# A Mamba block with a routed expert layer on one core: residual through TensorE, second layer norm on ScalarE

## The chip, the cores and the metric

The kernel runs on one core of one Trainium2 chip, as a single launch. Its metric is the device time in microseconds. Before the change it is 2424.81 us, the median of 3 runs (2423.86 to 2426.68).

## The reference, cut to what matters

The input is 4 sequences of 2048 tokens with 256 channels, all in float32. A selective scan with a residual is followed by a mixture of experts with a residual. In short:

```
h = layernorm(x) * (1 + ca) + sa
xs, res = split(h @ in_proj.T)                  # 512 + 512 channels
xs = silu(causal_conv4(xs) + conv_b)
dt, B, C = split(xs @ x_proj.T)                 # 64, 16, 16
delta = softplus(dt @ dt_proj.T + dt_b)
state = exp(delta * A) * state + delta * xs * B # 512 channels x 16 states, along the tokens
y = sum_n(state * C) * silu(res)
x = x + ga * (y @ out_proj.T)                   # the residual of this case
h = layernorm(x) * (1 + cb) + sb                # the second layer norm of this case
x = x + gb * moe(h)                             # 7 routed experts (top 1) and 1 shared
```

`layernorm(v)` is `(v - mean) / sqrt(var + 1e-5)` over the 256 channels.

## The kernel before, in words

There are two stages. The first, `fused_program`, walks the 8192 tokens in 16 chunks of 512; four chunks make one sequence. It does everything but the routed experts. The second, `experts_program`, handles 70 tiles of routed tokens and is not touched.

Within a chunk the 512 x 16 states are laid out as 16 sets of 4 groups, each group 128 partitions by 512 tokens, so a chunk has 64 scans of 128x512. For every group ScalarE makes `exp(delta * A)` into one of three PSUM banks `dA` (L850), VectorE scans it (L973), and after the four groups of a set ScalarE saves the last state (L865) and GpSimd multiplies the set by C (L1279). The input `delta * xs * B` of ten sets is multiplied by VectorE (L960), of the six others by GpSimd (L1272). TensorE sums over the states with a 0/1 matrix (L590). The states live in a ring of 8 sets.

All other work is put into this frame as items. Each item has a kind, an index and a chunk offset: offset 1 is work ahead for the next chunk, offset -1 is work for the chunk before. The kinds are: T and XS, RS, CV, XP, DT, DB (turn, input projection in two halves, convolution, x projection, delta), SUM (sum over states of 128 channels, and its gate by silu(res)), OP (output projection, two halves of 256 tokens), T2, RB, GL, GT (turn of the second norm, its copy back, logits), A and B and Y (shared expert), SU (Silu of the convolution), SRS (Silu of `res` and of the shared expert's gate), L0 and L1 (logarithms for softplus), N and N2 (normalize), LN and LN2 (layer norm sums), R and R2 (rsqrt), DU (delta times u), IN (input of a shared set), RC, G, G0, GM0, GM1 (the small gate arithmetic).

The order on each engine is written out by hand in five lists: `plan` for TensorE (one list of items per set), `evict` for ScalarE and `vector` for VectorE (one per group in a set), `gps` for GpSimd (one per set) and `transfers` for the DMA queue of SyncE. Each engine walks its list in order and waits on semaphores. TensorE's results go to three banks: kinds in `VECTOR` ("SUM", "OP", "DB", "A", "Y") use bank 2, the others alternate between banks 0 and 1; a bank is taken again when its last holder has been read.

What the change touches: the output projection puts 2 x 4 matmuls of 128x256 into bank 2 (L535). VectorE adds the residual `xres` to it, 128x512 at a time (`residual`, L989). When both halves are there, VectorE makes the statistics (`layernorm2`, bn_stats L928 and bn_aggr L934), GpSimd turns them into `rstd2` and `shift2` with a power of -0.5 (`rsqrt2`, L1250 to L1255), and ScalarE normalizes (`normalize2`, L780).

Since `dA` has three banks, exponential u waits for scan u - 3:

```
if u >= ABANK:
    act.wait_ge(scan_done, NG * NSET * c + u - ABANK + 1)
```

## Time and profile before

| | |
|---|---|
| median of 3 runs | 2424.81 us |
| the profiled execution's own time | 2425.52 us |
| its span, first to last instruction | 2423.7 us |
| mean granted TensorE clock | 0.917 |
| TensorE busy | 2129.3 us, 88% |
| GpSimd busy | 1979.4 us, 82% |
| VectorE busy | 1948.4 us, 80% |
| ScalarE busy | 1346.9 us, 56% |

PE is TensorE's matmuls, DVE is VectorE, ACT is ScalarE, POOL is GpSimd, SP is SyncE. A busy time is a sum over stages: the scan stage lies between about 60 and 1888 us, a short stage that settles the routing follows, and from about 1974 us the routed experts run, where TensorE is the one that works most. "L12" is line 12 of the kernel's file. A row of the timeline gives start, duration, engine, line and operation, how many of it follow each other, and in brackets how long the engine sat idle before it and who ended that.

### The profile page before, as it was taken

How to read it: one execution, taken by the hardware profiler on the slowest of the kernel's cores; microseconds unless marked ns; L12 is line 12 of the kernel's file. 1: busy time of each engine (PE TensorE's matmuls, PEld its weight loads, DVE VectorE, ACT ScalarE, POOL GpSimd, SP SyncE). 2: the span in 40 equal slices, each digit the busy share in tenths (PEclk: the TensorE clock that was granted, in tenths of full speed). 3: DMA queues.
4: the chain of work that ended last, by engine and by line, in shares of the span. 5: the costliest groups of instructions: out<-in, count | busy, mean ns of one | idle time of the engine just before them, and what ended most of it. 6: DMA issues, size and time to landing. Idle time of an engine off the chain costs nothing. (4 is left out here: it accounts for less than half of the span.)

```text
span 2423.7 us, 31216 instructions
## 1 busy us (share of the span) xinstructions
PE 2129.3 (88%) x7668; PEld 1007.6 (42%) x7669; DVE 1948.4 (80%) x2114; ACT 1346.9 (56%) x2391; POOL 1979.4 (82%) x858
## 2 busy tenths in 40 slices
PE   8859898988989898989898989889875779999998
PEld 3214343443434343434343334434332456666565
DVE  4889999999999999999999999999999832222222
ACT  4657666667585767666666667675745212222221
POOL 1999999999989999999998999999899445555553
PEclk9868999899989898989899899999887889999999
DMA  6433242424242324343242424242422512222221
GB/s 175 137 101 98 78 106 65 104 74 117 77 102 72 98 74 103 83 101 103 75 111 74 108 68 117 80 103 69 98 69 53 208 42 87 86 87 85 84 85 47
DMA packets 148360, 224.35 MB, mean 93 GB/s; under 512 B 47187, under 2 KB 84577, under 8 KB 144098
## 3 DMA queue, kind: packets, MB, share of 16 engines
q1 hardware_dynamic: 134818, 182.40, 28.8%
q0 software_dynamic: 13376, 40.12, 5.5%
q8 instruction: 57, 0.93, 0.2%
q14 instruction: 109, 0.89, 0.1%
HBM read 99.46 MB, written 31.45 MB: 54 GB/s over the span
## 5 line engine op out<-in xcount | busy, mean ns | idle before, releaser
L1279 POOL TENSOR_TENSOR ring<-ring,reps 128x2048 f32<-128x2048 f32 x256 | 1154.7, 4530 | 42.6 <-ACT state L865 42.6
L973 DVE TENSOR_TENSOR_SCAN ring<-dA,state,ring 128x512 f32<-128x512 f32 x768 | 929.7, 1262 | 13.5 <-ACT dA L850 9.2
L850 ACT ACTIVATE dA<-d_rep,a 128x512 f32<-128x512 f32 x1024 | 690.1, 686 | 433.1 <-DVE ring L973 426.4
L1272 POOL TENSOR_TENSOR ring<-u_rep,reps 128x2048 f32<-128x2048 f32 x96 | 436.2, 4544 | 44.6 <-PE bank L590 44.5
L960 DVE TENSOR_TENSOR ring<-u_ps,reps 128x2048 f32<-128x2048 f32 x160 | 360.5, 2269 | 8.8 <-issue 4.9
L590 PE MATMUL bank<-ring,spread 128*32 128x512 f32 x2048 | 283.2, 703 | 42.4 <-POOL ring L1279 37.8
L561 PE MATMUL bank<-n,w1s 128*128 128x512 f32 x512 | 266.1, 657 | 61.1 <-DVE delta L941 38.5
L973 DVE TENSOR_TENSOR_SCAN ring<-dA,ring 128x512 f32<-128x512 f32 x256 | 293.7, 1201 | 11.5 <-ACT dA L850 10.4
L1553 DVE TENSOR_TENSOR hid<-z,sg 128x512 f32<-128x512 f32 x70 | 48.4, 692 | 295.6 <-ACT sg L1530 295.6
L1468 PE MATMUL z<-ring,hT 128*128 x560 | 262.2, 612 | 3.6 <-issue 2.1
L516 PE MATMUL bank<-xin,w_in 128*128 128x512 f32 x512 | 244.9, 619 | 8.3 <-ACT xin L701 8.3
L520 PE MATMUL bank<-xpad,w_conv 128*128 128x512 f32 x496 | 224.0, 601 | 8.9 <-ACT us L716 8.8
L527 PE MATMUL bank<-xdbl,w_dt 65*128 65x512 f32 x256 | 149.0, 680 | 68.9 <-ACT n L732 52.1
L1435 POOL DMA_INDIRECT out<-outr,cur x70 | 70.9, 1013 | 145.2 <-DVE outr L1546 138.2
L561 PEld LDWEIGHTS bank<-n,w1s 128*128 128x128 f32 x512 | 98.2, 205 | 195.6 <-issue 93.2
L590 PEld LDWEIGHTS bank<-ring,spread 128*32 128x32 f32 x2048 | 69.9, 127 | 233.4 <-issue 213.2
L580 PE MATMUL u_ps<-us,spread 32*128 32x512 f32 x320 | 161.6, 705 | 0.0
L516 PEld LDWEIGHTS bank<-xin,w_in 128*128 128x128 f32 x512 | 99.6, 198 | 131.9 <-issue 119.2
L1468 PEld LDWEIGHTS z<-ring,hT 128*128 128x128 f32 x560 | 101.9, 192 | 122.4 <-issue 122.3
L1530 ACT ACTIVATE sg<-z 128x512 f32<-128x512 f32 x70 | 41.8, 597 | 199.5 <-PE z L1468 199.5
L520 PEld LDWEIGHTS bank<-xpad,w_conv 128*128 128x128 f32 x496 | 92.1, 190 | 132.5 <-issue 110.8
L1486 PE MATMUL y_ps<-reps,hidT 128*128 x560 | 132.4, 379 | 0.8 <-ACT hidT L1519 0.8
(237 smaller groups left out, 2456.7 us busy)
## 6 DMA issues: line engine op xcount, KB each, us to landing
d_rep<-delta SPq DMA_DIRECT2D x1024, 64.0 KB, 2.0
reps<-bc_rows SPq DMA_DIRECT2D x128, 256.0 KB, 6.3
u_rep<-us SPq DMA_DIRECT2D x384, 64.0 KB, 2.0
xres<-in_x SPq DMA_DIRECT2D x16, 512.0 KB, 3.6
token_rows<-xpad SPq DMA_DIRECT2D x32, 256.0 KB, 2.4
token_rows<-xres SPq DMA_DIRECT2D x16, 512.0 KB, 2.9
xin<-in_x SPq DMA_DIRECT2D x15, 512.0 KB, 9.4
ring<-in_w SPq DMA_DIRECT2D x7, 1024.0 KB, 14.5
```

What stands on the lines that cost most here:

```text
L516: last = nc.tensor.matmul(ps_[:, :], t["w_in"][:, k, col:col + P], hT[:, k, :], start=(k == 0), stop=(k == KD - 1))
L520: last = nc.tensor.matmul(ps_[:, :], t["w_conv"][:, j, k, :], xpad[:, j, k:k + T], start=(k == 0), stop=(k == KCONV - 1))
L527: last = nc.tensor.matmul(ps_[:, :], t["w_dt"][:, j * P:(j + 1) * P], xdbl[0:DT_ROWS, :], start=True, stop=True)
L561: last = nc.tensor.matmul(ps_[:, :], t["w1s"][:, k, col:col + P], h2T[:, k, :], start=(k == 0), stop=(k == KD - 1))
L580: nc.tensor.matmul(u_ps[:, i % 2, :], t["spread"][DS * q:DS * q + DS].rearrange("p f d -> p (f d)"), us[DS * q:DS * q + DS, par, j, :], st ...
L590: last = nc.tensor.matmul(ps_[DS * q:DS * q + DS, :], t["gather"], hs[:, (SPC * j + q) % RING, n, :], start=(n == 0), stop=(n == NG - 1), ...
L850: nc.scalar.activation(dA[:, u % ABANK, :], d_rep[:, q, :], ACT.Exp, scale=t["a"][:, u:u + 1]).then_inc(da_ready, 1)
L960: nc.vector.tensor_tensor(hs[:, s % RING], u_ps[:, i % 2, :].unsqueeze(1).to_broadcast([P, NG, T]), b_rep[:, par, :].rearrange("p (g t) -> ...
L973: nc.vector.tensor_tensor_scan(hs[:, s % RING, g, :], dA[:, u % ABANK, :], hs[:, s % RING, g, :], state[:, u:u + 1] if m else 0.0, ALU.mul ...
L1272: nc.gpsimd.tensor_tensor(hs[:, s % RING], u_rep[:, i % UBUF, :].unsqueeze(1).to_broadcast([P, NG, T]), b_rep[:, par, :].rearrange("p (g t ...
L1279: nc.gpsimd.tensor_tensor(hs[:, s % RING, :, :], hs[:, s % RING, :, :], c_rep[:, par, :].rearrange("p (g t) -> p g t", g=NG), ALU.mult).th ...
L1468: last = nc.tensor.matmul(z[:, q % 2, half, :], hT[:, q % 2, i, :], t["w1r"][:, e, i, half * H:(half + 1) * H], start=(i == 0), stop=(i == ...
```

## The change

The residual is added by TensorE: each half of a projection begins with a matmul of the identity by `xres`, and the 4 matmuls of the projection accumulate onto it. Its bank is read by ScalarE, which writes the new `xres` and, as a second output, the sum of each row. ScalarE then does the rest of the second layer norm as well: `squares2` (VS0, VS1) makes the negative mean and the sum of squared deviations, `deviation2` (V2) makes rstd by Ln and Exp and the shift. VectorE's `residual` and `layernorm2` and GpSimd's `rsqrt2` go. All five lists get a new order, the six shared sets stay the same. In the part behind the last chunk, VectorE's first routing steps stand together behind SUM 3.

```diff
+                        pe.wait_ge(xres_loaded, 16 * f + 16)
                     for h in range(2):
+                        tt = 2 * j + h
+                        nc.tensor.matmul(ps_[:, h * D:(h + 1) * D], t["ident"][:], xres[:, tt, :], start=True, stop=False)
                         for k in range(KI):
-                            tt = 2 * j + h
                             last = nc.tensor.matmul(ps_[:, h * D:(h + 1) * D], res[:, (par + off) % 2, k, tt * P:(tt + 1) * P], t["w_out"][:, k, :],
-                                                    start=(k == 0), stop=(k == KI - 1))
+                                                    start=False, stop=(k == KI - 1))
...
+                elif kind == "OP":
+                    for h in range(2):
+                        tt = 2 * j + h
+                        last = nc.scalar.activation(xres[:, tt, :], ps_[:, h * D:(h + 1) * D], ACT.Copy, accum_out=sum2[:, tt:tt + 1])
+                    last.then_inc(x1_ready, 1)
...
+            def squares2(f, j):
+                part = slice(2 * j, 2 * j + 2)
+                act.wait_ge(x1_ready, 2 * f + j + 1)
+                nc.scalar.activation(nmean2[:, part], sum2[:, part], ACT.Copy, scale=-1.0 / D).then_inc(ln2_step, 1)
+                act.wait_ge(ln2_step, 2 * f + j + 1)
+                if not (known(f) and f == 0):
+                    act.wait_ge(a_made, KI * f)
+                for tt in range(2 * j, 2 * j + 2):
+                    last = nc.scalar.activation(n2[:, tt, :], xres[:, tt, :], ACT.Square, bias=nmean2[:, tt:tt + 1], accum_out=var2[:, tt:tt + 1])
+                last.then_inc(stats2_ready, 1)
+            def deviation2(f):
+                act.wait_ge(stats2_ready, 2 * f + 2)
+                nc.scalar.activation(rstd2, var2, ACT.Ln, bias=eps2[:, 0:1], scale=1.0 / D).then_inc(rstd2_step, 1)
+                act.wait_ge(rstd2_step, 2 * f + 1)
+                nc.scalar.activation(rstd2, rstd2, ACT.Exp, scale=-0.5).then_inc(rstd2_step, 1)
+                act.wait_ge(rstd2_step, 2 * f + 2)
+                for tt in range(TT):
+                    last = nc.scalar.activation(shift2[:, tt:tt + 1], nmean2[:, tt:tt + 1], ACT.Copy, scale=rstd2[:, tt:tt + 1])
+                last.then_inc(shift2_ready, 1)
...
-            5: [[], [], [(('CV', 3), 1)], []],
-            6: [[(('SU', 0), 1)], [], [(('HALO', 0), 2), (('RS', 0), 1)], []],
+            5: [[(('VS0', 0), -1)], [], [(('CV', 3), 1), (('SU', 0), 1)], []],
+            6: [[(('OP', 1), -1)], [], [], []],
...
-            def layernorm2(f):
...
-            def residual(f, j):
...
-            def rsqrt2(f):
```

What stands on ScalarE in chunk 1, around the Silu of the convolution (`us<-us 128x2048`). The rows `dA<-d_rep,a` are exponentials, `state<-ring` is the save behind the third of a set, `us<-bank1,cb` the eviction of a convolution, `xpad<-xpad` the halo. Before:

```order
L850 ACTIVATE dA<-d_rep,a 128x512 x3
L716 ACTIVATE us<-bank1,cb 128x512
L865 ACTIVATE state<-ring 128x4
L850 ACTIVATE dA<-d_rep,a 128x512 x2
L753 ACT_TABLE_LOAD
L753 ACTIVATE us<-us 128x2048
L764 ACT_TABLE_LOAD
L850 ACTIVATE dA<-d_rep,a 128x512 x2
```

And now:

```order
L734 ACTIVATE xres,ln2<-bank2 128x256 x2
L881 ACTIVATE dA<-d_rep,a 128x512
L786 ACTIVATE ln2<-ln2 128x2
L791 ACTIVATE n2,ln2<-xres,ln2 128x256 x2
L881 ACTIVATE dA<-d_rep,a 128x512 x2
L718 ACTIVATE us<-bank1,cb 128x512
L760 ACT_TABLE_LOAD
L760 ACTIVATE us<-us 128x2048
L771 ACT_TABLE_LOAD
L896 ACTIVATE state<-ring 128x4
```

The Silu with its two table loads moved from behind exponential 24 (the first of set 6) to behind exponential 22 (the third of set 5), into one gap with the eviction of the last convolution; the eviction of projection 0 and the first two Squares stand before it.

What stands on VectorE in chunk 1 between the gates of SUM 1 and SUM 2 (`res<-bank2,res`). `stats<-xin` is the first layer norm, which stays, `delta<-delta,bank2` are DB 0 and DB 1, `xpad<-bank2,xpad` the hidden product A. Before:

```order
L982 TENSOR_TENSOR res<-bank2,res 128x512
L916 BN_STATS stats<-xin 128x6 x4
L922 BN_AGGR mv<-stats 128x2 x4
L973 SCALAR_TENSOR_TENSOR ring<-dA,state,ring 128x512 x5
L941 SCALAR_TENSOR_TENSOR delta<-delta,bank2 128x512
L973 SCALAR_TENSOR_TENSOR ring<-dA,state,ring 128x512
L960 TENSOR_TENSOR ring<-u_ps,reps 128x2048
L973 SCALAR_TENSOR_TENSOR ring<-dA,state,ring 128x512
L941 SCALAR_TENSOR_TENSOR delta<-delta,bank2 128x512
L973 SCALAR_TENSOR_TENSOR ring<-dA,state,ring 128x512 x3
L996 TENSOR_TENSOR xpad<-bank2,xpad 128x512
```

And now:

```order
L1001 TENSOR_TENSOR res<-bank2,res 128x512
L992 SCALAR_TENSOR_TENSOR ring<-dA,state,ring 128x512 x4
L947 BN_STATS stats<-xin 128x6 x4
L953 BN_AGGR mv<-stats 128x2 x4
L960 SCALAR_TENSOR_TENSOR delta<-delta,bank2 128x512
L992 SCALAR_TENSOR_TENSOR ring<-dA,state,ring 128x512
L960 SCALAR_TENSOR_TENSOR delta<-delta,bank2 128x512
L979 TENSOR_TENSOR ring<-u_ps,reps 128x2048
L992 SCALAR_TENSOR_TENSOR ring<-dA,state,ring 128x512 x2
L1007 TENSOR_TENSOR xpad<-bank2,xpad 128x512
```

The first layer norm moved five scans later, and the first hidden product two scans earlier; both now stand in the stretch in which ScalarE does its two other Silus (SRS, behind exponential 49).

What stands on TensorE in chunk 1 between the third convolution and the second projection. Before (`w_out,res` is a projection, `xpad,w_conv` are convolutions of 4 matmuls each, `u_ps` the spread of an input):

```order
L535 MATMUL bank<-w_out,res 128x256 x8
L520 MATMUL bank<-xpad,w_conv 128x512 x8
L535 MATMUL bank<-w_out,res 128x256 x8
```

And now:

```order
L535 MATMUL bank<-xres,ident 128x256
L537 MATMUL bank<-w_out,res 128x256 x4
L535 MATMUL bank<-xres,ident 128x256
L537 MATMUL bank<-w_out,res 128x256 x4
L582 MATMUL u_ps<-us,spread 128x512
L520 MATMUL bank<-xpad,w_conv 128x512 x4
L516 MATMUL bank<-xin,w_in 128x512 x2
```

One convolution moved ahead of projection 0; the last one still stands behind it, and a projection of the next kind (`w_in`) stands between it and projection 1.

## Rows read from the trace of the kernel before

**Rows 1.** The page: the span, and section 1.

```profile
span 2423.7 us, 31216 instructions
PE 2129.3 (88%) x7668; PEld 1007.6 (42%) x7669; DVE 1948.4 (80%) x2114; ACT 1346.9 (56%) x2391; POOL 1979.4 (82%) x858
```

**Rows 2.** Window: busy us of PE, PEld, DVE, ACT, POOL; clock, DMA.

```profile
215.50:1820.90 1605.40, 1429.36 (x5170) 619.63 (x5166) 1544.96 (x1534) 1070.94 (x1890) 1498.77 (x459) 0.91 0.35 90
```

**Rows 3.** VectorE's waits, same window: us in total, times, longest.

```profile
DVE res L982 <- PE bank L590: 26.0, 22, 1.7
DVE ring L973 <- ACT dA L850: 11.2, 16, 1.4
...
DVE ring L960 <- issue: 4.9, 2, 2.6
```

**Rows 4.** VectorE's timeline: second layer norm of chunks 1 and 15.

```profile
215.51 1.38 DVE L928 BATCH_NORM_STATS2 stats<-xres 128x6 f32<-128x256 f32 x4
...
1820.90 1.38 DVE L928 BATCH_NORM_STATS2 stats<-xres 128x6 f32<-128x256 f32 x4
```

**Rows 5.** VectorE's timeline, chunk 9 (from 1087.58), a row of chunk 8 ahead.

```profile
1011.46 4.55 DVE L973 TENSOR_TENSOR_SCAN ring<-dA,ring 128x512 f32<-128x512 f32 x4
...
1087.58 4.48 DVE L960 TENSOR_TENSOR ring<-u_ps,reps 128x2048 f32<-128x2048 f32 x2
...
1122.76 0.66 DVE L989 TENSOR_TENSOR xres<-bank,xres 128x512 f32<-128x512 f32 x1
1123.34 2.28 DVE L960 TENSOR_TENSOR ring<-u_ps,reps 128x2048 f32<-128x2048 f32 x1
...
1132.03 1.38 DVE L928 BATCH_NORM_STATS2 stats<-xres 128x6 f32<-128x256 f32 x4
...
1133.98 5.98 DVE L973 TENSOR_TENSOR_SCAN ring<-dA,state,ring 128x512 f32<-128x512 f32 x5
...
1178.69 2.46 DVE L973 TENSOR_TENSOR_SCAN ring<-dA,state,ring 128x512 f32<-128x512 f32 x2 [0.57 <-ACT dA L850]
```

**Rows 6.** GpSimd's timeline, chunk 9.

```profile
1134.24 0.23 POOL L1250 TENSOR_SCALAR mv<-mv 128x4 f32<-128x4 f32 x1 [1.21 <-DVE mv L934]
...
1136.37 4.53 POOL L1279 TENSOR_TENSOR ring<-ring,reps 128x2048 f32<-128x2048 f32 x1
...
1162.42 4.53 POOL L1272 TENSOR_TENSOR ring<-u_rep,reps 128x2048 f32<-128x2048 f32 x1 [3.56 <-PE bank L590]
```

**Rows 7.** GpSimd by lines: busy us, mean ns, idle before.

```profile
L1246 POOL TENSOR_TENSOR us<-delta,us 128x1024 f32<-128x1024 f32 x30 | 71.1, 2369 | 0.0
```

**Rows 8.** TensorE's timeline, chunk 9.

```profile
1112.89 3.72 PE L535 MATMUL bank<-w_out,res 128*128 128x256 f32 x16
...
1120.70 3.70 PE L520 MATMUL bank<-xpad,w_conv 128*128 128x512 f32 x8 [0.65 <-ACT us L716]
1124.24 3.62 PE L535 MATMUL bank<-w_out,res 128*128 128x256 f32 x16
```

**Rows 9.** ScalarE's timeline, chunk 9.

```profile
1124.44 0.69 ACT L716 ACTIVATE us<-bank,cb 128x512 f32<-128x512 f32 x1 [0.87 <-PE bank L520]
...
1128.73 1.28 ACT L753 ACT_TABLE_LOAD   x1
...
1131.96 1.28 ACT L764 ACT_TABLE_LOAD   x1
1133.25 1.30 ACT L850 ACTIVATE dA<-d_rep,a 128x512 f32<-128x512 f32 x2
```

**Rows 10.** ScalarE by lines: busy us, mean ns, idle before.

```profile
L780 ACT ACTIVATE n<-xres,shift,rstd 128x256 f32<-128x256 f32 x64 | 33.1, 591 | 20.1 <-POOL shift L1255 20.1
L791 ACT ACTIVATE gs<-gs 128x1 f32<-128x1 f32 x128 | 26.9, 280 | 2.1 <-DVE gs L1003 2.1
L1513 ACT ACTIVATE hT<-t_ps 128x256 f32<-128x256 f32 x70 | 26.4, 378 | 40.0 <-PE t_ps L1458 40.0
...
L785 ACT ACTIVATE gs<-gs 128x4 f32<-128x4 f32 x16 | 3.0, 190 | 0.0
```

124 lines of the change are left out of this document (49 added, 75 removed), and 28 rows, old and new, of the table evict.

## The prediction, on record before the result

> **What bounds the kernel now.** I read the page first. The span is 2423.7 us; VectorE is busy 80% of it, GpSimd 82%, TensorE 88% and ScalarE 56% [rows 1]. The chain that ended last tells only of the experts' stage at the end, which the change does not touch, so I asked for the windows of the scan stage: in 1605.40 us VectorE is busy 1544.96 (96%), GpSimd 1498.77 (93%), TensorE 1429.36 at a granted clock of 0.91, and ScalarE 1070.94 (67%) [rows 2]. VectorE is the nearest to full, GpSimd next.
>
> The second view is VectorE's timeline. The four sums of squares of the second layer norm start at 215.51 and at 1820.90 with 14 chunks between them, so a chunk takes 114.67 us on average [rows 4]. The third is VectorE's waits in that stretch: 26.0 us for the sum over states (L590), 11.2 for ScalarE's exponentials and 4.9 of issue [rows 3]. All that is not busy in rows 2 is 60.4 us, 4.3 per chunk; the other 110.4 us of a chunk are instructions of VectorE end to end. A microsecond taken off VectorE is therefore worth a microsecond, as long as nobody makes it wait instead.
>
> **What goes.** On VectorE the first residual add takes 1122.76 to 1123.34, 0.58 us from start to start, and the second the same; bn_stats and bn_aggr take 1132.03 to 1133.98, 1.95 us with the wait between them [rows 5]. That is 3.11 us per chunk. On GpSimd the four small operations hold the queue from 1134.24 to 1136.37, 2.13 us, after 1.21 us of waiting [rows 6]; GpSimd has as much less to do as VectorE, so it does not become the bound by this. The items carry offset -1 in the lists, so chunks 1 to 15 of 16 have them in the stage, and the sixteenth set stands behind the last scan.
>
> **What comes on TensorE.** Two identity matmuls in each of the two output projections. A projection of 8 matmuls is 16 records in 3.6 us [rows 8], 0.23 per record, so 10 matmuls take 4.5 us: 0.9 us more each, 1.8 per chunk. TensorE is idle 176 us in 14 chunks [rows 2], 12.6 per chunk, which hides it, except where a projection stands ahead of something urgent (below).
>
> **What comes on ScalarE.** Per chunk: four evictions of 128x256 with a running sum, four Square of 128x256 with a bias and a sum, two scalings of 128x2, a Ln and an Exp of 128x4, and four 128x1 products. The nearest rows are 0.38 us for a 128x256 Copy from a bank, 0.59 for the 128x256 Identity with two column operands, 0.19 for 128x4, 0.28 for 128x1 [rows 10]. No row shows an ACTIVATE that also writes a sum. Its bounds are the plain row below (0.38) and twice the plain row above (0.8 and 1.2); I take 0.38 and 0.50, nearest to the plain rows. Sum: 1.5 + 2.0 + 0.4 + 0.4 + 0.9 = 5.2 us, with self-waits some 5.7. ScalarE has 534 us of idle in the 14 chunks [rows 2], 38 per chunk, so the average says that it is free. The average is not the test: dA has three banks, so an exponential can be started only when the scan three before it is done, and each gap between two exponentials holds only what VectorE does in that time.
>
> I walked each gap. Count from the first multiply of a chunk (1087.58 [rows 5]).
>
> The costly gap is in set 5. The Silu of the convolution moves from behind exponential 24 to behind exponential 22, together with the last convolution's eviction. In the old place it hid: VectorE did four scans, a residual add and bn_stats/bn_aggr beside it. Now: TensorE ends the last convolution at 36.66 (1124.24 [rows 8]); less its wait of 0.65, plus 0.9 for the identity matmuls in projection 0, which is still ahead of it, 36.9. The eviction starts 0.2 later as it did before (1124.24 to 1124.44) and ends at 37.7; table load, Silu and table load take 1128.73 to 1133.25, 4.52 [rows 9], to 42.2; save and exponential 23 end at 43.0. ScalarE's own new work ahead of that (eviction of projection 0 at 33, two Squares, exponentials 20 to 22) ends at about 37.2, so the two meet. VectorE needs that exponential at: end of set 4, 35.18 (1122.76), plus 2.2 for the multiply (two take 4.48 at 1087.58), plus three scans of 1.18 (five take 5.98 with 0.09 of overlap left off), 40.9 [rows 5]. Stall 2.1 us. In chunks that begin a batch four scans take 4.55, so one 1.14 or less; 23 of them are 0.9 us earlier, stall 3.0. Over 11 and 4 chunks: 2.3 us each.
>
> The other long gap, in set 7 (eviction, Ln, Exp, four products, projection eviction, normalize, eviction: about 5.2 us), lies beside three scans, one gating and two 128x2048 multiplies, 8.7 us less two exponentials: 7.1 of room. It fits. The gap with the two Silus in set 12 stalls VectorE 0.57 now (1178.69 [rows 5]). The first layer norm (about 1.95) and the first hidden product (0.58) move beside it, so this stall goes: 11.2 us over 14 chunks is 0.8 each. The wait for the sum over states is 1.86 each. SUM 1 is read one scan (1.18) later, SUM 2 stands behind the layer norm as well, and GpSimd comes to both with 2.13 less behind it; I keep 0.3 and count 1.56 as gained.
>
> **The sum.** Off: 3.11 + 0.8 + 1.56 = 5.47. On: 2.34. Net 3.13 per chunk, times 15 is 47.0 us. The first chunk has none of these items and waits for GpSimd's start. Behind the last scan VectorE's routing steps and the small gate operations move by 2 us in both directions; I take zero. The profiled execution took 2425.52 against a median of 2424.81, 0.7 more. 2425.5 - 47.0 = 2378.5, and 2377.8 on the scale of the median: 2378.
>
> **A rule against the change.** By the rows a table load costs 1.28 and the next instruction begins at once (1131.96 + 1.28, then 1133.25 [rows 9]). The Trainium skill (ScalarE: Activation LUTs, What ACT_TABLE_LOAD costs) says that each switch also drains the engine for about 1.38 us, 2.66 in all. By that rule the gap in set 5 would be 2.8 us longer and the sum would leave 0.3 us per chunk, about 2420. The trace disagrees: no such time stands on either side of the loads, so it has a chance of 0.01, within the case of no change below.
>
> **Rivals.**
> 1. The lump hides. If TensorE or ScalarE comes to the last convolution earlier than in my walk, the stall in set 5 is small, and up to 5.47 per chunk are gained: 82 us, 2343. For: all other waits were moved behind cover. Against: the convolution's end is a plain sum of TensorE's rows, with no idle time left in it.
> 2. GpSimd holds the chunk. It carries 22 multiplies of 4.5 us (16 by C, 6 shared sets [rows 6]), two products of 2.37 [rows 7] and the first norm's chain of 2.1 like the one that goes, 106 of a chunk that I put at 111.5. A first state's save late in set 0 and the wait of its gate operation for the logits cost it time (that operation now stands ahead of a 128x2048 multiply). If 2 us more than before are lost, 1.1 per chunk remain: 17 us, about 2408. For: it was 93% busy. Against: its longest wait, for SUM 1 ahead of that multiply (3.6 us, 1162.42 [rows 6]), ends earlier.
> 3. ScalarE loses its lead, the case on the other side. The place is from the eviction of projection 0 to exponential 31; the price is that of an ACTIVATE that also writes a sum. At twice the plain row, 1.8 us more stand ahead of exponential 23; exponentials 25 and 30, behind the second eviction and the second two Squares, have lead for the plain rows only and lose 0.4 and 0.6 by my walk. 2.8 added to 2.34 eats 5.1 of 5.47: 2420. From 2.1 times (3.13 against 2.8) it decides. At 2.5 times the added stalls are 4.2, a loss of 1.1 per chunk: 2442. For: no row prices it. Against: every ACTIVATE row follows its size.
> 4. The residual's new load order (xres is now read by TensorE, about as late in the chunk as VectorE read it before) delays projection 0: the load takes 3.6 us and is issued some 10 us ahead. I give it no case of its own.
>
> **Chances.** Forecast 0.62 (its own range 2362 to 2395), rival 1 0.13, rival 2 0.12: faster, 0.87. Rival 3 at twice the row, with the drain: within 0.2%, 4.8 us, which is about what a measurement of this kernel can tell from no change, 0.04. Rival 3 above that: slower, 0.09. The range for 8 in 10 goes from 2349, short of the far end of rival 1, to 2409, just past rival 2; rival 3 is left out.
>
> **What would show it.** In the new profile: VectorE about 1898 us busy (1948.4 less 16 times 3.11), no row of bn_stats on xres; VectorE's wait for ScalarE's exponentials up from 19.6 us in all to about 45, nearly all ahead of the fourth scan of set 5, in lumps of 2 to 3 us; its wait for L590's sums down from 38.2 to about 15; a chunk at 111.5 us instead of 114.7; the eviction with sum at 0.38 and Square at 0.50. I am wrong if a chunk stays above 113 us, if ACTIVATE with a sum costs twice its plain row, or if GpSimd's wait column falls to nothing while VectorE still waits.

## The result and the profile after

The changed kernel takes 2452.69 us (median of 4, 2447.82 to 2460.72) against 2424.79 for the kernel before (median of 4). The ratio is 1.012, 95% interval 1.009 to 1.015: slower, where 2378 was forecast. Its four executions lie 13 us apart, those of the kernel before 3 us. The profiled execution took 2447.82.

The page, span and section 1, against [rows 1]:

```profile
span 2446.1 us, 31534 instructions
PE 2200.1 (90%) x7796; PEld 1045.0 (43%) x7797; DVE 1908.4 (78%) x1954; ACT 1437.7 (59%) x2775; POOL 1954.4 (80%) x795
```

VectorE has 40.0 us less to do, as wanted, and the span is 22.4 us longer, so VectorE is idle 62.4 us more. Its waits over the whole span of the kernel after (what it did, who ended the wait, us in all, times, longest):

```profile
DVE xpad L1007 <- PE bank L563: 56.5, 24, 3.7
DVE ring L992 <- ACT dA L881: 54.6, 30, 3.4
...
DVE delta L960 <- PE bank L527: 10.0, 8, 2.5
DVE delta L960 <- ACT delta L756: 8.5, 2, 4.3
DVE d_rep L1157 <- PE u_ps L660: 8.4, 1, 8.4
...
DVE res L1001 <- PE bank L592: 4.7, 3, 2.2
```

And the same view of the kernel before:

```profile
DVE res L982 <- PE bank L590: 38.2, 26, 4.9
...
DVE ring L973 <- ACT dA L850: 19.6, 21, 4.7
...
DVE delta L941 <- PE bank L527: 3.7, 3, 1.9
...
DVE xpad L996 <- PE bank L561: 3.4, 2, 2.2
...
DVE delta L941 <- ACT delta L749: 3.4, 1, 3.4
```

| VectorE waits for | before | after | change |
|---|---|---|---|
| the shared expert's hidden product (item A) | 3.4 | 56.5 | +53.1 |
| ScalarE's exponentials | 19.6 | 54.6 | +35.0 |
| sums over states | 38.2 | 4.7 | -33.5 |
| the count of the routing | 0 | 8.4 | +8.4 |
| delta's bank and logarithm | 7.1 | 18.5 | +11.4 |
| small ones | | | -12.0 |

The 53.1 us of the first line are more than the 47 that the change was to bring. Two of the other lines were in the forecast: the sums (-33.5) and most of the exponentials.

The time is lost in the middle of the scan stage. From the bn_stats at 250.4 to the one at 1650.2 lie 12 chunks of 116.65 us; before, from 245.7 to 1620.6, they were 114.57, so 24.9 us are lost there. (The two starts do not compare with each other, since bn_stats stands five scans later in the new list.) By the first scan of a chunk, the kernel after is 0.8 us ahead in the second chunk (175.61 against 176.41) and 25.8 us behind in the last (1806.82 against 1781.02). The last chunk takes 101.8 us instead of 107.0, so 20.6 us are left at the last scan's end (1908.59 against 1888.01). In the last chunk VectorE waits neither for the products A nor for exponential 23; it prepares no next chunk, so it has no Silu of a convolution.

What the hidden products wait for can be read from one timeline of all engines, chunk of 950.5 (kernel after; start, duration, engine, in brackets the idle time before):

```profile
952.51 0.68 DVE L960 SCALAR_TENSOR_TENSOR delta<-delta,bank 128x512 f32<-128x512 f32 x1
...
953.24 1.13 PE L527 MATMUL bank<-xdbl,w_dt 65*128 65x512 f32 x2 [0.95 <-DVE delta L960]
954.30 1.79 PE L582 MATMUL u_ps<-us,spread 32*128 32x512 f32 x2
...
956.02 3.78 PE L527 MATMUL bank<-xdbl,w_dt 65*128 65x512 f32 x4
...
959.60 2.80 PE L563 MATMUL bank<-n,w1s 128*128 128x512 f32 x4
...
962.44 0.69 DVE L1007 TENSOR_TENSOR xpad<-bank,xpad 128x512 f32<-128x512 f32 x1 [2.47 <-PE bank L563]
...
971.85 3.58 PE L563 MATMUL bank<-n,w1s 128*128 128x512 f32 x4 [3.40 <-DVE res L1001]
...
975.47 0.69 DVE L1007 TENSOR_TENSOR xpad<-bank,xpad 128x512 f32<-128x512 f32 x1 [1.31 <-PE bank L563]
```

The layer norm moved ahead of VectorE's read of DB 0 (952.51). DB 1, in the same bank, waits for that read. Behind DB 1 the list has the spread of u, DT 2 and DT 3, and then A 0, which VectorE now asks for two scans earlier than before: it waits 2.47 us. A 1 waits for the read of sum 2 and starts after 3.40 us of idleness; its four matmuls take 3.58 us, more than the two scans beside them (2.45), and VectorE waits again.

The same place in the kernel before, chunk 9:

```profile
1176.97 3.78 PE L561 MATMUL bank<-n,w1s 128*128 128x512 f32 x4 [2.86 <-DVE delta L941]
...
1181.06 0.66 DVE L996 TENSOR_TENSOR xpad<-bank,xpad 128x512 f32<-128x512 f32 x1
```

Counted from the chunk's first scan (1091.97 before, 874.83 after), TensorE starts A 0 at 85.0 us before and at 84.8 after, the same. VectorE came for it at 89.1 before and is ready for it at 85.1 after (two scans from 957.51). TensorE did not get slower there; the reader comes 4 us earlier and the maker does not. The granted clock of these stretches (busy us of PE, PEld, DVE, ACT, POOL, then clock, DMA share, GB/s):

```profile
953.20:962.40 9.20, 9.16 (x12) 3.04 (x12) 6.53 (x5) 9.07 (x12) 8.67 (x6) 0.63 0.12 30
971.80:975.40 3.60, 3.55 (x5) 1.21 (x5) 2.36 (x2) 2.17 (x5) 3.60 (x1) 0.54 0.69 175
976.40:981.40 5.00, 4.96 (x11) 1.65 (x10) 5.00 (x5) 3.18 (x5) 5.00 (x2) 1.00 1.02 218
```

0.54 is mostly the lower of the two levels (1.2 GHz), 1.00 the upper (2.4 GHz). In this chunk the stretches at the lower one follow idleness of TensorE, of 0.95 and 3.40 us. At the upper level four such matmuls take 1.98 us. The kernel before (windows below) went through its A 1 to A 3 at 1.00; its A 0 ran at the lower level too, but VectorE asked for it later:

```profile
1176.90:1180.70 3.80, 3.73 (x5) 1.19 (x5) 3.23 (x4) 3.79 (x7) 3.16 (x2) 0.50 0.31 76
1188.40:1199.40 11.00, 9.90 (x25) 4.40 (x26) 11.00 (x13) 7.35 (x16) 11.00 (x4) 1.00 0.30 74
```

Of the 14 chunks with such products, seven look like the one above: A 0 partly at the upper level, VectorE waits 2.5 to 2.7 us for it, then TensorE is idle 3.0 to 4.6 us ahead of A 1, A 1 is slow, and VectorE waits 1.3 to 1.5 us more. The seven others look like this one:

```profile
847.61 0.69 DVE L1007 TENSOR_TENSOR xpad<-bank,xpad 128x512 f32<-128x512 f32 x1 [3.57 <-PE bank L563]
...
857.02 1.98 PE L563 MATMUL bank<-n,w1s 128*128 128x512 f32 x4 [2.51 <-DVE res L1001]
```

A 0 is at the lower level throughout (four matmuls in 3.62 us), VectorE waits 3.4 to 3.7 us, TensorE is idle 2.4 to 2.7 us ahead of A 1, and A 1 passes at the upper level without a wait. Either way a chunk loses 3.4 to 4.2 us here.

The stall at exponential 23 is where the walk had put it. ScalarE and VectorE, kernel after, against [rows 9]:

```profile
908.04 3.62 DVE L992 TENSOR_TENSOR_SCAN ring<-dA,state,ring 128x512 f32<-128x512 f32 x3
...
908.49 0.69 ACT L718 ACTIVATE us<-bank,cb 128x512 f32<-128x512 f32 x1 [0.83 <-PE bank L520]
909.20 1.28 ACT L760 ACT_TABLE_LOAD   x1
...
912.42 1.28 ACT L771 ACT_TABLE_LOAD   x1
...
913.83 1.28 ACT L881 ACTIVATE dA<-d_rep,a 128x512 f32<-128x512 f32 x2
...
914.54 5.98 DVE L992 TENSOR_TENSOR_SCAN ring<-dA,state,ring 128x512 f32<-128x512 f32 x5 [2.87 <-ACT dA L881]
```

It is 2.87 us in most chunks, where 2.1 was forecast, and 3.44 in those that begin a sequence, which wait 1.03 and 0.49 elsewhere too (3.0 was forecast). The sums themselves cost what was taken; by ScalarE's lines (busy us, mean ns), against [rows 10]:

```profile
L791 ACT ACTIVATE n<-xres,ln 128x256 f32<-128x256 f32 x64 | 32.0, 500 | 1.3
L734 ACT ACTIVATE xres<-bank 128x256 f32<-128x256 f32 x64 | 23.5, 372 | 28.2 <-PE bank L537 28.2
...
L734 ACT ACTIVATION_READ_ACCUMULATOR xres<-bank 128x1 f32 x64 | 12.6, 196 | 0.0
L791 ACT ACTIVATION_READ_ACCUMULATOR n<-xres,ln 128x1 f32 x64 | 11.9, 186 | 0.0
```

0.37 and 0.50 us, plus a separate short instruction that reads the sum, of which about 0.1 us shows as distance to the next start (905.89, 906.29, 906.38 in one chunk).

### The profile page after: what moved, and what is told of

The parts are those of the page before. It is cut to its first block and busy times, and to the rows that moved or that the text cites. A ratio compares the mean times of both kernels' runs of the same rounds, so it can differ in the third digit from the quotient of the medians.

```text
span 2446.1 us, 31534 instructions
## 1 busy us (share of the span) xinstructions
PE 2200.1 (90%) x7796; PEld 1045.0 (43%) x7797; DVE 1908.4 (78%) x1954; ACT 1437.7 (59%) x2775; POOL 1954.4 (80%) x795
## 5 line engine op out<-in xcount | busy, mean ns | idle before, releaser
L1276 POOL TENSOR_TENSOR ring<-ring,reps 128x2048 f32<-128x2048 f32 x256 | 1157.0, 4534 | 125.1 <-ACT state L896 124.5
L992 DVE TENSOR_TENSOR_SCAN ring<-dA,state,ring 128x512 f32<-128x512 f32 x768 | 927.9, 1264 | 37.6 <-ACT dA L881 33.1
L979 DVE TENSOR_TENSOR ring<-u_ps,reps 128x2048 f32<-128x2048 f32 x160 | 361.2, 2274 | 6.9 <-issue 4.7
L592 PE MATMUL bank<-ring,spread 128*32 128x512 f32 x2048 | 272.8, 680 | 42.1 <-POOL ring L1276 33.0
L563 PE MATMUL bank<-n,w1s 128*128 128x512 f32 x512 | 269.5, 669 | 44.6 <-DVE res L1001 42.6
L527 PE MATMUL bank<-xdbl,w_dt 65*128 65x512 f32 x256 | 183.8, 824 | 50.0 <-DVE delta L960 25.8
L582 PE MATMUL u_ps<-us,spread 32*128 32x512 f32 x320 | 190.3, 694 | 0.0
L563 PEld LDWEIGHTS bank<-n,w1s 128*128 128x128 f32 x512 | 104.3, 214 | 184.5 <-issue 111.6
L592 PEld LDWEIGHTS bank<-ring,spread 128*32 128x32 f32 x2048 | 69.6, 126 | 237.8 <-issue 201.0
L1464 PEld LDWEIGHTS z<-ring,hT 128*128 128x128 f32 x560 | 101.8, 192 | 121.5 <-issue 121.4
L571 PE MATMUL bank<-w2s,xpad 128*128 128x256 f32 x512 | 120.1, 388 | 24.3 <-DVE xpad L1007 13.7
```

The lines of the kernel that those rows point to most:

```text
L527: last = nc.tensor.matmul(ps_[:, :], t["w_dt"][:, j * P:(j + 1) * P], xdbl[0:DT_ROWS, :], start=True, stop=True)
L563: last = nc.tensor.matmul(ps_[:, :], t["w1s"][:, k, col:col + P], h2T[:, k, :], start=(k == 0), stop=(k == KD - 1))
L582: nc.tensor.matmul(u_ps[:, i % 2, :], t["spread"][DS * q:DS * q + DS].rearrange("p f d -> p (f d)"), us[DS * q:DS * q + DS, par, j, :], st ...
L592: last = nc.tensor.matmul(ps_[DS * q:DS * q + DS, :], t["gather"], hs[:, (SPC * j + q) % RING, n, :], start=(n == 0), stop=(n == NG - 1), ...
L979: nc.vector.tensor_tensor(hs[:, s % RING], u_ps[:, i % 2, :].unsqueeze(1).to_broadcast([P, NG, T]), b_rep[:, par, :].rearrange("p (g t) -> ...
L992: nc.vector.tensor_tensor_scan(hs[:, s % RING, g, :], dA[:, u % ABANK, :], hs[:, s % RING, g, :], state[:, u:u + 1] if m else 0.0, ALU.mul ...
```

## The experiments

The first theory, formed from the trace: the replaced lists cost the time, by the place of A 0 and of the Silu; its rival: the new operations cost it, whatever the order.

### One place at a time

**a0_back**, VectorE reads A 0 where it did before:

```
-            12: [[], [(('A', 0), -1)], [], []],
+            12: [[], [], [], [(('A', 0), -1)]],
```

> The changed kernel, with VectorE's first hidden product back behind the fourth scan of set 12 instead of the second; nothing else moved. Theory 1 (the lists cost the time): in the changed kernel TensorE reaches this product 2.5 us late, about 37 of the 56.5 us of VectorE's waits for L563. Those go, the 20 us ahead of the second product stay: 2452.7 - 37 = 2416 us, and the wait for L563 at about 20 us. Theory 2 (the new operations cost it, by what ScalarE's sums and TensorE's identity products load on their engines): the wait only moves to the next exponential, 2450 +- 4 us. Forecast by theory 1: 2416, range 2405 to 2430.

Measured: 2414.69 us, ratio to before 0.996 (0.994 to 0.998). As forecast, 38.0 us less than the changed kernel, and less than the kernel before. VectorE's wait for L563 is 21.3 us. One entry in one list changes the sign of the result.

**su_back**, the Silu behind exponential 24 again:

```
-            5: ... [(('CV', 3), 1), (('SU', 0), 1)], []],
-            6: [[(('OP', 1), -1)], ...
+            5: ... [(('CV', 3), 1)], []],
+            6: [[(('SU', 0), 1), (('OP', 1), -1)], ...
```

> The changed kernel, with the Silu of the convolution (and its two table loads) back behind exponential 24, as before; the convolution's last eviction stays behind exponential 22. Theory 1: the stall at exponential 23 (2.9 us in most chunks, 5.0 in those that begin a batch, 3.4 on average, times 15 = 51 us) falls to what an eviction alone costs; the Silu now has four scans beside it but no residual add and no layer norm, so some 1 us of stall is left: 2452.7 - 36 = 2417 us, VectorE's wait for exponentials down from 54.6 to about 20. Theory 2: ScalarE is short of time by its new operations wherever the Silu stands, the stall moves to exponential 25 to 28 and the time stays at 2450 +- 5. Forecast 2417, range 2405 to 2440.

Measured: 2471.68 us, ratio 1.019 (1.018 to 1.021). A miss by 55 us. The stall only moved: VectorE waits 3.2 to 3.4 us behind the Silu there. The rest came at the hidden products, 76.0 us instead of 56.5. In two chunks TensorE stayed at its lower level through all of them:

```profile
511.66 3.78 PE L563 MATMUL bank<-n,w1s 128*128 128x512 f32 x4 [4.36 <-DVE res L1001]
...
515.37 2.07 PE L582 MATMUL u_ps<-us,spread 32*128 32x512 f32 x2
...
515.48 0.69 DVE L1007 TENSOR_TENSOR xpad<-bank,xpad 128x512 f32<-128x512 f32 x1 [1.51 <-PE bank L563]
...
517.37 3.78 PE L563 MATMUL bank<-n,w1s 128*128 128x512 f32 x4
...
521.20 0.69 DVE L1007 TENSOR_TENSOR xpad<-bank,xpad 128x512 f32<-128x512 f32 x1 [2.66 <-PE bank L563]
...
526.90 0.69 DVE L1007 TENSOR_TENSOR xpad<-bank,xpad 128x512 f32<-128x512 f32 x1 [2.65 <-PE bank L563]
```

```profile
511.60:526.90 15.30, 15.20 (x16) 4.52 (x16) 8.48 (x10) 6.05 (x11) 15.30 (x4) 0.51 0.50 107
```

TensorE is busy 15.20 of these 15.30 us, at 0.51. Between two products stands a spread of u, so one turn takes it 3.72 + 2.00 = 5.72 us at the lower level, while VectorE is through a read and two scans in 3.06: it waits the difference, 2.66 at A 2 and 2.65 at A 3. At the upper level TensorE's turn is 1.92 + 1.05 = 2.97 (976.41 to 979.38 in the changed kernel), and VectorE's is 2.97 too (978.44 to 981.41), without a wait. The two chunks took 122.9 and 124.3 us. Neither theory gave the time: the stall moved as theory 2 says, but the rest is the hidden products' wait, 19.5 us more.

**banks_back**, order of DT 1 and RB 0 on TensorE. Banks 0 and 1 are dealt out by the place in `plan`; in the changed list DT 0 and DT 1 share bank 1:

```
-            9: [(('DT', 0), 1), (('RB', 0), -1), (('DT', 1), 1), (('RB', 1), -1), ...
+            9: [(('DT', 0), 1), (('DT', 1), 1), (('RB', 0), -1), (('RB', 1), -1), ...
```

> The changed kernel, with TensorE's order of four items back: second decay projection ahead of the first turned-back rows (DT 0, DT 1, RB 0, RB 1 instead of DT 0, RB 0, DT 1, RB 1). Banks are dealt out by the place in this list, so the first two decay projections get different banks again. Theory: in the changed kernel they share one, so at the start the second waits for ScalarE to read the first, and VectorE's first multiply starts at 61.5 us instead of 56.1. With the order back it starts at about 56.1 and the whole is 5.4 us shorter: 2447 us, nothing else changed. Rival: the start is hidden behind GpSimd's scaling of weights or a load, the later stages catch up, and the time stays at 2452.7 +- 2.

Measured: 2479.09 us (2463.63 to 2496.86), ratio 1.025 (1.021 to 1.029). The first multiply starts at 56.10 instead of 61.51, as forecast, but VectorE then waits 3.13 and 1.09 us for exponentials and 2.47 for a sum, and the first layer norm of the stage starts at 141.5 (140.6 in the changed kernel). The gain at the start is gone before the second chunk. The hidden products waited 64.5 us, 10.3 in one chunk, and the executions lie 33 us apart.

### The operations

**ops_old_order**, the changed kernel's operations with the lists of before; what is new gets a place:

```
evict 5: [[(('OP', 0), -1)], [(('VS0', 0), -1)], [(('CV', 3), 1)], []],
evict 6: [[(('OP', 1), -1), (('SU', 0), 1)], [], ...
evict 7: [[(('VS1', 0), -1)], [], ..., [(('V2', 0), -1), (('XP', 0), 1), ...
```

> All operations of the changed kernel with the lists of the kernel before; only what must have a new place gets one (evictions with sums behind exponentials 20 and 24, Squares behind 21 and 28, the deviation behind 31). Theory 1: the operations are worth what was forecast for VectorE's busy time, 3.1 us per chunk, and lose about 1 us per chunk where the Silu behind exponential 24 has lost the residual add and the layer norm that covered it; the waits for sums over states (38 us) stay: 2425 - 47 + 15 = 2393 us, range 2380 to 2410. Theory 2: ScalarE and TensorE cannot carry them, 2425 or more.

Measured: 2440.38 us, ratio 1.007 (1.005 to 1.009). Theory 1 gave 2393. The hidden products wait 3.4 us, as before; sums 37.6, as before; exponentials 78.5 instead of 19.6. In most chunks the stall behind Silu and projection 1 is 3.95 us, where the kernel before has none. VectorE's busy time is 44 us less and its waits for exponentials are 59 more, and 15 us is what it is slower by. Is that lost cover or ScalarE's added work?

**vec_cut** tells how much the cover is, on the kernel before: VectorE's work is taken out, nothing is added elsewhere. The residual add keeps 4 of 256 columns and the layer norm's statistics become two fills.

```
-                nc.vector.tensor_tensor(xres[:, 2 * j:2 * j + 2, :], ...
+                nc.vector.tensor_tensor(xres[:, 2 * j:2 * j + 2, 0:4], ...
-                    last = nc.vector.bn_stats(stats[:, tt, :], xres[:, tt, :])
+                nc.vector.memset(stats[:, 0, 0:4], 1.0).then_inc(ln2_step, 1)
-                    last = nc.vector.bn_aggr(mv2[:, tt, :], stats[:, tt, :])
+                nc.vector.memset(mv2[:], 1.0).then_inc(stats2_ready, 1)
```

> The kernel before with its own lists, from which VectorE's part is nearly taken out and given to no other engine: the residual add works on 4 of 256 columns, and the four bn_stats and four bn_aggr are two small fills (the second layer norm works with constants, and most of the residual is left out). TensorE and ScalarE do exactly what they did. VectorE has about 2.5 us per chunk less to do. Theory 1 (in the old order these instructions were the cover of the Silu behind exponential 24): a stall of 2 to 3 us appears there and most of the gain is given back, 2410 to 2422. Theory 2 (VectorE's busy time is the price, and ScalarE's new operations are what made ops_old_order slow): 2424.8 - 15 x 2.5 = 2387.

Measured: 2423.38 us against 2424.14, ratio 1.000 (0.999 to 1.001). VectorE is busy 1907.9 us, 40.5 less, and not a microsecond is gained. Its waits:

```profile
DVE ring L969 <- ACT dA L850: 47.8, 34, 4.5
```

and the place, behind the Silu, where there was no stall:

```profile
667.49 1.28 ACT L753 ACT_TABLE_LOAD   x1
...
670.71 1.28 ACT L764 ACT_TABLE_LOAD   x1
...
672.73 5.98 DVE L969 TENSOR_TENSOR_SCAN ring<-dA,state,ring 128x512 f32<-128x512 f32 x5 [2.01 <-ACT dA L850]
```

So in the old lists these instructions were cover for ScalarE's Silu: 28.2 of the 40.5 us come back as waits for exponentials and 8.1 as waits ahead of VectorE's multiplies (L956). The profiled execution is 3.6 us shorter than that of the kernel before; the medians differ by 0.8 only.

Cover is not all of it. In ops_old_order the stall at the same place is 3.95 us, not 2.01, the waits for exponentials are 30.7 us longer, and the kernel is some 17 us slower than vec_cut. There the eviction of projection 1 stands ahead of the table load and starts after a wait of 0.64 us for TensorE (674.71), so the load comes 1.5 us after exponential 24 has ended, where in vec_cut it comes at once. In the old order the new operations on ScalarE and TensorE thus cost about as much again as the lost cover. Both theories of vec_cut's expectation hold in part, though its time fits only the first (it lies 1.4 us above that range).

**no_ident**, without the identity matmuls (the residual is left out):

```
-                        nc.tensor.matmul(ps_[...], t["ident"][:], xres[:, tt, :], start=True, stop=False)
```

> The changed kernel without the four identity matmuls of a chunk; the residual is left out of the result. Theory A (TensorE's added work is on the path, since the last convolution stands behind the first projection and ScalarE waits for it): the last convolution ends 0.9 us earlier, the stall at exponential 23 falls by 0.9, 15 x 0.9 = 13 us less, 2439. Theory B (the work is hidden, the order alone costs): within 3 us of 2452.7. The products' waits can add swings of 5 us either way.

Measured: 2459.67 us, ratio 1.015 (1.012 to 1.018). The stall at exponential 23 falls as theory A says, from 2.87 to 2.01 us in most chunks, 54.6 to 43.0 in all. It is eaten by the hidden products, 71.0 us instead of 56.5. Theory A has the stall right and the time wrong by 21 us. Less work for TensorE made the kernel no faster.

**no_sums**, without the running sums (the second layer norm works with constants):

```
-  ... ACT.Copy, accum_out=sum2[:, tt:tt + 1])
-  ... ACT.Square, bias=nmean2[:, tt:tt + 1], accum_out=var2[:, tt:tt + 1])
```

> The changed kernel without the running sums: the four evictions and four Squares of a chunk write no sum (the second layer norm then works with constants), and their eight separate readings of the accumulator, 0.19 us each by the trace, go. Theory 1 (the sums are no cause): ScalarE is 8 x 0.1 to 0.19 = 0.8 to 1.5 us per chunk shorter, ScalarE waits for the last convolution anyway, and the time stays within 4 us of 2452.7. Theory 2 (my third rival, sums eat ScalarE's lead): 1.5 us per chunk come back at exponentials 23 to 30, 2430.

Measured: 2455.42 us, ratio 1.012 (1.011 to 1.014). Theory 1: VectorE waits 54.7 us for exponentials, as with the sums, and the stall at exponential 23 is 2.87 us as in the changed kernel. The ACTIVATEs themselves last the same without their sums (374 and 500 ns on average against 372 and 500). Rival 3 of the prediction is false in its price; of its places, exponentials 25 and 30 show no wait of VectorE in the changed kernel's trace.

The run also gives a measure of chance: the wait for the hidden products is 64.7 us here instead of 56.5, though nothing of TensorE's list was touched. A difference of some 8 us in that wait between two traces says nothing about an edit.

### The hidden products

**awake** adds transposes on TensorE in the idle stretch ahead of A 1:

```
+                    if j == 0 and not (known(c) and c == -1):
+                        for i in range(4 * TT):
+                            tt = i % TT
+                            last = nc.tensor.transpose(ps_[...], xin[:, tt, ...], t["ident"][:])
```

> The changed kernel, with 16 more transposes (the same ones again, into the same bank) behind the first group of each chunk's transposes, which stand on TensorE ahead of the second hidden product. Theory 1 (TensorE comes to the second product at its lower clock after an idle stretch of 3.4 us, so its four matmuls take 3.6 us instead of 2.0, and VectorE stalls 1.2 us there, and further on at the third and fourth in some chunks): with 2.6 us of that stretch filled the four matmuls take 2.0 us and the stall at the second product goes, 15 times 1.2 = 18 us: 2435, range 2428 to 2442, and the executions lie closer together than the 13 us of the changed kernel. Theory 2 (the bank, not the clock: the product waits for VectorE's read and is late at any clock): the same time or 1 to 3 us more by the added work, 2453 to 2456.

Measured: 2450.81 us, ratio 1.011 (1.009 to 1.012). Half a result; the forecast of 2435 was missed. In the changed kernel VectorE waits 1.3 to 1.5 us for A 1 in seven of fourteen chunks; here 1.3 to 1.4 us in two, 0.1 to 0.8 in four and not at all in eight. But in four chunks it now waits 2.2 to 2.7 us for A 2, which it did in no chunk of the changed kernel's trace, and its wait for the products is 64.3 us in all. In the eight chunks without a wait the idle stretch ahead of A 1 was 0.7 to 1.7 us and A 1 ran at 1.00; in the six others 2.3 to 3.9 us were left of it, and A 1 ran at 0.54 to 0.80. So the transposes filled the stretch in some chunks only, and the changed kernel's A 1 had kept the upper level after 2.4 to 2.7 us. What decides between the levels there is left open.

**a_first** moves A 0 on TensorE instead of on VectorE:

```
-            12: [(('DT', 2), 1), (('DT', 3), 1)],
-            13: [(('A', 0), -1), (('SUM', 2), 0), ...
+            12: [(('A', 0), -1), (('DT', 2), 1), (('DT', 3), 1)],
+            13: [(('SUM', 2), 0), ...
```

> The changed kernel with one item moved on TensorE: the first hidden product ahead of the decay projections 2 and 3 instead of behind them; VectorE still reads it behind the second scan of set 12. Theory 1 (the product stands behind work that nobody waits for yet): it starts at the end of the spread of u, 3.6 us earlier, and is done about when VectorE comes, so VectorE's wait ahead of the first product (2.5 to 3.6 us in every chunk, 43 us) goes to 0.3 or less, the one at the second (1.3 us in half the chunks) stays: 2452.7 - 40 = 2413, range 2403 to 2425. Theory 2 (only VectorE's place matters; TensorE is late there because its order has already lost the time): 2440 or more.

Measured: 2412.1 us (10 runs, 2407.07 to 2425.42), ratio 0.995 (0.994 to 0.997). As forecast, 40.6 us less. The wait ahead of A 0 is 0 to 0.4 us in every chunk read. So the cause is the pair of places: VectorE's went forward, and TensorE's did not go with it. Mending either one (a0_back, a_first) makes the kernel faster than the kernel before.

**a_first_back** takes both moves:

> Both moves of the first hidden product: ahead of the decay projections 2 and 3 on TensorE, and behind the fourth scan of set 12 on VectorE. Against the run with VectorE's place alone (2414.7, which kept 1.2 us of wait per chunk there): no wait is left, 2414.7 - 15 x 1.2 = 2397, range 2390 to 2408; VectorE's wait for L563 5 us or less. Rival: the sum over states 2 or the product behind it comes later instead and takes it back, 2412 to 2416.

Measured: 2404.22 us (2403.11 to 2406.03), ratio 0.992 (0.990 to 0.993), the fastest of all, 20.6 us less than the kernel before. It lies above the 2397 of the forecast and within its range. Its waits:

```profile
DVE ring L992 <- ACT dA L881: 53.6, 27, 3.4
...
DVE res L1001 <- PE bank L592: 14.5, 11, 2.6
DVE delta L960 <- PE bank L527: 11.5, 14, 2.5
...
DVE xpad L1007 <- PE bank L563: 5.7, 4, 2.3
```

The rival had a part: sum 2 stands behind DT 2 and DT 3 as ever, A 0 has left, and VectorE waits for it 0.7 to 1.9 us in seven chunks.

**banks_a_back** is a_first_back with the bank order of banks_back:

> The bank order of banks_back (2479, with executions from 2464 to 2497) together with both moves of the first hidden product of a_first_back (2404). Theory 1 (the slowness and the wide spread of banks_back come through the hidden products, late and at TensorE's lower clock in some chunks, and have nothing to do with the banks): 2404 +- 5, executions within 5 us, VectorE's wait for L563 below 12 us. Theory 2 (the bank order itself is worse, since the turned-back rows come later): 2425 or more.

Measured: 2415.7 us (9 runs, 2412.94 to 2418.02), ratio 0.997 (0.996 to 0.998). Between the two theories. The spread is gone (5 us instead of 33) and so is the wait for the products. banks_back was 26.4 us slower than the changed kernel; with the pair of places mended the bank order costs 11.5 us against a_first_back, in waits for exponentials (60.8) and sums (22.2). So somewhat more than half of its price came through the products, and the rest is its own.

### The Silu

**conv_first** puts the last convolution ahead of the first output projection and the Silu behind exponential 23 (A 0 as in a0_back):

```
plan 3: [(('CV', 2), 1), (('CV', 3), 1), (('OP', 0), -1)],
evict 5: [[(('CV', 3), 1)], [(('OP', 0), -1)], [], [(('SU', 0), 1)]],
evict 6: [[], [(('VS0', 0), -1)], [(('OP', 1), -1)], []],
```

> The changed kernel with three places changed: VectorE's first hidden product behind the fourth scan of set 12 (as in the run that did this alone, 2414.7); TensorE's last convolution ahead of the first output projection; on ScalarE the last convolution's eviction behind exponential 20, the first projection's behind 21, the Silu behind 23 (its three scans and the multiply of set 6 give 5.8 us of cover for 5.2), first Squares and second projection's eviction behind 25 and 26. Theory 1: the stall at exponential 23 (2.9 us, 4.7 in chunks that begin a batch) goes to 0.5 or less: 2414.7 - 15 x 2.8 = 2373 us, range 2362 to 2388, and VectorE waits 15 us or less for exponentials in the chunks. Theory 2 (ScalarE has no lead left with its new work, wherever the Silu stands, as the run with the Silu behind 24 showed no gain): the stall moves on and the time stays above 2400.

Measured: 2487.25 us, ratio 1.026 (1.024 to 1.028). A miss by 114 us. VectorE waits 2.35 us in each chunk for the spread of u for set 6, which stands behind the convolution and the whole projection in TensorE's list (43.5 us in all for such spreads), and the stall behind the Silu is 2.46: VectorE's multiply for set 6 comes before scan 20, not beside exponentials 21 to 23 as I had it.

**conv_mid** leaves that spread ahead, puts the Silu behind exponential 21, and the projections' evictions behind 24 and 28; A 0 as in a_first_back:

```
plan 4: [(('CV', 3), 1), (('OP', 0), -1), (('RS', 0), 1), ...
evict 5: [[(('CV', 3), 1)], [(('SU', 0), 1)], [], []],
evict 6: [[(('OP', 0), -1)], [], [(('VS0', 0), -1)], []],
evict 7: [[(('OP', 1), -1)], [(('RS', 0), 1)], [(('VS1', 0), -1)], [(('RS', 1), 1), ...
```

> Both moves of the first hidden product, and TensorE's last convolution ahead of the first output projection but behind the spread of u for set 6 (which the run with the convolution further up had held back by 2.4 us). On ScalarE the last convolution's eviction goes behind exponential 20 and the Silu behind 21, beside VectorE's multiply for set 6; first projection's eviction behind 24, first Squares behind 26, second eviction behind 28, residual gate's first eviction behind 29, second Squares behind 30; VectorE's read of sum 0 one scan later. Theory 1 (the stall at exponential 23 is the late end of the last convolution on TensorE, 2.9 to 4.5 us): the convolution ends 4.4 us earlier, 5.8 us of VectorE's work stand beside 5.3 of ScalarE's, and the stall goes to 0.5: 2397 - 15 x 2.6 = 2358, range 2348 to 2375. Theory 2 (ScalarE has no lead left with its new work): the waits go to exponentials 25 to 34 and the time stays above 2390.

Measured: 2458.33 us, ratio 1.014 (1.012 to 1.016). The stall at the Silu is gone, 0.28 us are left of it,

```profile
1145.54 8.33 DVE L992 TENSOR_TENSOR_SCAN ring<-dA,state,ring 128x512 f32<-128x512 f32 x7 [0.28 <-ACT dA L881]
...
1147.63 1.07 PE L535 MATMUL bank<-xres,ident 128*128 128x256 f32 x2 [2.69 <-ACT xres L734]
...
1153.94 0.38 ACT L734 ACTIVATE xres<-bank 128x256 f32<-128x256 f32 x1 [2.63 <-PE bank L537]
```

but the late evictions keep the one bank that the projections share with the sums. The second projection waits 2.69 us for it, ScalarE 2.63 for the second projection, and behind both sum 0 holds back VectorE's multiplies (43.8 us for L592 and L582 ahead of L979).

**silu_beside** moves those evictions to behind 23 and 26:

```
evict 5: [[(('CV', 3), 1)], [(('SU', 0), 1)], [], [(('OP', 0), -1)]],
evict 6: [[], [], [(('OP', 1), -1)], [(('RS', 0), 1)]],
evict 7: [[(('VS0', 0), -1)], [], [(('VS1', 0), -1)], [(('RS', 1), 1), ...
```

> As conv_mid (both moves of the first hidden product; last convolution ahead of the first output projection; Silu behind exponential 21), but the evictions of the output projections come earlier on ScalarE, behind exponentials 23 and 26 instead of 24 and 28, the Squares behind 28 and 30, and VectorE reads sum 0 where the changed kernel does. Theory 1: conv_mid took the stall at exponential 23 away (2.9 us down to 0.3) and lost on the bank of the second projection, which held back sum 0 and VectorE's multiply for sets 8 and 9 by 2.9 us. With the bank free two exponentials earlier, that wait is under 0.5 us, and ScalarE loses some 1.5 us in lumps at exponentials 24, 29 and 31: 2404.2 - 15 x 1.3 = 2385, range 2372 to 2400. Theory 2 (ScalarE cannot carry the new operations between exponentials 22 and 32, where VectorE has scans alone, in any order): VectorE's waits for exponentials stay at 54 us or more and the time at 2404 or more.

Measured: 2451.88 us (2439.5 to 2456.83), ratio 1.013 (1.011 to 1.014). Now ScalarE asks too early:

```profile
1148.02 0.38 ACT L734 ACTIVATE xres<-bank 128x256 f32<-128x256 f32 x1 [4.56 <-PE bank L537]
```

and stops its exponentials with it; VectorE then waits 3.36 us in this chunk, 1.5 to 3.7 in the others (85.6 in all for exponentials). Of theory 2 only this stands: each of the three orders is slower than the one it was made from, conv_first by 72.6 us against a0_back, conv_mid by 54.1 and silu_beside by 47.7 against a_first_back. That no order does better is not shown.

**count_first** moves one step of the routing behind the last scan:

```
-  PLACES = {("OP", 0): [(count, 0)], ...
+  PLACES = {("SUM", 3): [(count, 0)], ...
```

> As a_first_back (2404.2), with one step of the routing behind the last scan moved on TensorE: the counting matmuls of the first part stand behind the last sum over states instead of behind the first output projection. Theory 1 (the changed kernel lets VectorE wait 8.4 us once for that count, behind ten matmuls of the projection and ScalarE's eviction, and the tail is longer by it): the wait falls to about 2 us and the whole is 3 to 6 us shorter, 2400. Rival (the tail is set by the experts' weights or by ScalarE's second table): no change, 2404 +- 1.5.

Measured: 2406.22 us (2401.89 to 2412.01), ratio 0.994 (0.992 to 0.995). The rival is right: the wait for the count is gone, a new one of 6.4 us for ScalarE's logits stands a little later, and nothing is gained.

## Why the prediction was wrong

**What failed.** The step "The first layer norm (about 1.95) and the first hidden product (0.58) move beside it, so this stall goes: 11.2 us over 14 chunks is 0.8 each". The stall did go. But I looked only at the engine that reads. By reading A 0 two scans earlier VectorE came to it 4 us earlier in the chunk, and TensorE made it at the same time as before. On the way there TensorE even waits 0.95 us for the read of DB 0, ahead of which the layer norm now stands. Waits of 3.8 us per chunk took the place of 0.8. a0_back (38.0 us), a_first (40.6) and both together (48.5) show it: with the pair mended the time is 2404.2, within the range 2349 to 2409. I had TensorE's list at hand and its idle time of 12.6 us per chunk; the average said that it is free, and I trusted it on TensorE after having refused it on ScalarE.

The pair is not the whole gap to 2378. Even a_first_back stays 26 us above it: its waits for exponentials are 53.6 us where 45 were forecast, those for delta (bank and logarithm) 20.0 where 7.1 had been and no change was counted, the count behind the last scan is 7.0, and VectorE's busy time fell by 42.8 instead of 50. The sums gave what was forecast (23.7 against 23.4).

**VectorE's work, 3.11 per chunk.** Roughly right in size: 40.0 us of busy time less, where 50 were forecast (1898, measured 1908.4). The 3.11 hold the wait between bn_stats and bn_aggr, 3.9 us in all, which is no busy time; the rest of the gap is in scans and the others, which are a little longer. Its worth was the premise "a microsecond taken off VectorE is therefore worth a microsecond, as long as nobody makes it wait instead". vec_cut shows how much hangs on the second half: in the old order it was worth nothing.

**The stall at exponential 23, 2.34 per chunk.** Right in place, short in size: 2.87 us in most chunks. VectorE's waits for exponentials came to 54.6 us, 45 were forecast. The walk redone on the chunk of 870.43 (its first multiply): ScalarE's own work ends at 37.2, as forecast; TensorE's last convolution ends at 37.9, where the walk had 36.9; exponential 23 is done at 44.1 instead of 43.0, and VectorE is ready at 41.2 instead of 40.9. The walk took TensorE's rows of the old list. There two spreads of u stand together and take 1.24 us to the next row (1099.96); in the new list they stand apart and take 1.05 us each (881.10 and 884.07). no_ident shows that the identity matmuls, which were counted, make 0.86 of the 2.87.

**The sums over states, 1.56 per chunk.** Right in kind and too small: 33.5 us over the whole, 23.4 were forecast. In a_first_back it is 23.7: with the products' wait gone, some 10 us of the waits for sums come back.

**The operations on ScalarE.** 0.37 and 0.50 us; 0.38 and 0.50 were forecast. Rival 3 (chance 0.09 for slower) came true in its sign and in nothing else; no_sums takes its mechanism away and the stalls stay. Rival 2 did not happen: GpSimd waited 124.5 us for the states that ScalarE saves, where it had waited 42.6, and no wait of VectorE's in the trace is for GpSimd.

**The start and the tail, taken as zero.** The start was not: DT 0 and DT 1 share a bank by the new order, and the first multiply is 5.4 us later. banks_back shows that it is worth nothing to mend it. In the tail a wait of 8.4 us for the count is new; with it taken away in count_first, another of 6.4 us appears behind it and nothing is gained.

**The drain rule** of the Trainium skill (ScalarE: Activation LUTs, What ACT_TABLE_LOAD costs), 1.38 us beside each load: the trace of after disagrees as that of before did. From 909.20 to the Silu and from 912.42 to the next instruction lie 1.29 and 1.30 us, the load itself.

**The chances.** Slower had 0.09, all of it on a price of ScalarE. All five lists were replaced, and no rival was given to a pair of places that no longer fit each other. Such a case should have had most of what I gave to the forecast.

Left open: why the products pass at the upper level in some chunks and at the lower in others (3.57 and 0, or 2.47 and 1.3, or 10.3 us in a chunk); whether that is also why the executions of the changed kernel scatter, which is likely but not shown; and whether an order of the Silu exists that keeps the operations' gain.

## What to carry to other kernels

When a change moves the reader of a result, look up where its maker stands in its own queue and what that queue waits for, in the same walk; an engine that is idle a tenth of the time can still be late at every single meeting. Work taken off the busiest engine is worth its time only where no other engine was hiding a lump behind it: find the lump first (here a Silu between two table loads), and ask what will cover it afterwards. And where two engines work in turns, compare the turn at both levels of TensorE's clock: here TensorE's is 2.97 us at the upper level, just as long as VectorE's, and 5.72 at the lower, so the place has no slack for a slow stretch.
